# Nine output slots for the experts' rows in place of three, and one set of load semaphores for two stages

## The reference, cut to what matters

```python
xn = _layernorm(x, axis=-1)
x = x + gnn(xn, edge_index, edge_attr_64, ...) + mix(xn[None], ...)[0]   # segment sums + MLP; 4 layers of linear attention + MLP
x = x + ffn(_layernorm(x, axis=-1)[None], ...)[0]
```

```python
logits = xf @ router_w.T + router_b
idx = jnp.argmax(logits, axis=-1)
w1t = jnp.take(W1, idx, axis=0)
h = jnp.einsum('nd,ndh->nh', xf, w1t) + jnp.take(b1, idx, axis=0)      # 256 -> 64
h = jax.nn.relu(h)
w2t = jnp.take(W2, idx, axis=0)
out = jnp.einsum('nh,nhd->nd', h, w2t) + jnp.take(b2, idx, axis=0)     # 64 -> 256
out = jax.nn.relu(out)
```

## Time and profile before

| | |
|---|---|
| Runs before, us | 3072.39, 3080.54, 3084.48; median 3080.54 |
| Time of the profiled execution, us | 3077.36 |
| Its span, us | 3075.2 |
| Busy, share of the span | PE 88%, DVE 69%, ACT 50%, POOL 56% |
| Mean granted clock of PE | 0.938 |
| Stage of the experts' segments | about 2880 to the end |

### The profile page before, as it was taken

How to read it: one execution, slowest core, us unless ns; L and a number is a source line. 1 busy time by engine, 2 the same in 40 slices (tenths; PEclk the granted TensorE clock), 3 DMA queues, 4 the chain that set the end, 5 groups by cost and what they waited for, 6 DMA issues and landing times.

```text
span 3075.2 us, 56118 instructions
## 1 busy us (share of the span) xinstructions
PE 2715.3 (88%) x18842; PEld 2482.9 (81%) x18842; DVE 2125.2 (69%) x4836; ACT 1528.0 (50%) x2947; POOL 1723.8 (56%) x1611
## 2 busy tenths in 40 slices
PE   4888899999979999997999999788888888992597
PEld 2666799999978999996889999688888888992465
DVE  8887567677756666675567767688888886893144
ACT  0333366666635566662565666344444445771254
POOL 0011178777758888885888885154454553224455
PEclk7898899999989999998999999799999998996688
DMA  3000223323232223223223221233323322201332
GB/s 119 24 27 25 82 50 68 68 61 64 54 93 66 63 68 65 59 62 95 64 59 68 65 64 43 64 108 84 87 81 87 82 81 60 59 25 50 85 100 76
DMA packets 255488, 207.87 MB, mean 68 GB/s; under 512 B 165433, under 2 KB 194314, under 8 KB 255205
## 3 DMA queue, kind: packets, MB, share of 16 engines
q1 hardware_dynamic: 197606, 162.55, 19.7%
q0 software_dynamic: 57600, 41.75, 7.0%
HBM read 136.93 MB, written 70.16 MB: 67 GB/s over the span
## 4 chain that ended last, share of the span: by engine, by line
PE 18%; POOL 13%; issue 8%; DVE 7%; DMA 4%; ACT 2%; DVEq 1%; SPq 0%; POOLq 0%; ACTq 0%
PE bank L375 16%; POOL edges_sorted L725 8%; DMA nodes_out<-orow,oidx 3%; POOL tokens_sorted L790 2%; DVE xh L1266 2%; PE bank L1808 1%; DVE hidh_lo L1302 1%; DMA staging<-in_edge_attr 1%; POOL r L703 1%; DVE oh L1494 1%; POOL ehl L742 1%; DVE bn L1257 1%; ACT hidh_hi L837 1%; ACT ehl L913 1%; ACT hid L831 0%
## 5 line engine op out<-in xcount | busy, mean ns | idle before, releaser
L725 POOL DMA_INDIRECT edges_sorted<-staging,pos_i x850 | 1058.2, 1245 | 254.2 <-issue 230.8
L831 ACT ACTIVATE hid<-bank,b1p 128x250 f32<-128x250 f32 x800 | 331.9, 466 | 388.0 <-PE bank L375 385.8
L375 PE MATMUL bank<-h_hi,w_hi 128*128 128x250 f32 x1600 | 482.7, 302 | 19.7 <-DVE h_lo L1286 19.7
L1302 DVE TENSOR_TENSOR hidh_lo<-hid,hidh_hi 128x500 fp32r<-128x500 f32 x400 | 296.9, 742 | 272.6 <-ACT hidh_hi L837 265.1
L375 PE MATMUL bank<-w_hi,hidh_hi 128*125 128x256 f32 x1600 | 468.1, 293 | 0.0
L375 PE MATMUL bank<-h_hi,w_lo 128*128 128x250 f32 x1600 | 451.1, 282 | 0.0
L375 PE MATMUL bank<-w_hi,hidh_lo 128*125 128x256 f32 x1600 | 450.9, 282 | 0.0
L375 PE MATMUL bank<-w_lo,hidh_hi 128*125 128x256 f32 x1600 | 449.8, 281 | 0.0
L375 PE MATMUL bank<-h_lo,w_hi 128*128 128x250 f32 x1600 | 448.0, 280 | 0.0
L375 PE MATMUL bank<-wqk,h 128*125 128x256 f32 x1600 | 380.6, 392 | 0.6 <-ACT mbc L882 0.6
L375 PEld LDWEIGHTS bank<-wqk,h 128*125 128x125 f32 x1600 | 306.3, 195 | 47.4 <-issue 1.2
(11 more groups left out here) (289 smaller groups left out, 5754.5 us busy)
## 6 DMA issues: line engine op xcount, KB each, us to landing
staging<-edges_sorted SPq DMA_DIRECT2D x103, 260.0 KB, 2.7
staging<-in_edge_attr SPq DMA_DIRECT2D x50, 531.2 KB
queries<-qn SPq DMA_DIRECT2D x100, 250.0 KB
qin<-queries SPq DMA_DIRECT2D x100, 250.0 KB
edges_sorted<-staging,pos_i POOLq DMA_INDIRECT x850, 3.7
rows_in<-edges_sorted SPq DMA_DIRECT2D x50, 260.0 KB, 2.7
yin<-tokens_sorted SPq DMA_DIRECT2D x81, 127.0 KB
raw<-in_L_mix_W SPq DMA_DIRECT2D x8, 1024.0 KB, 6.3
```

The source lines that it names most:

```text
L375: return nc.tensor.matmul(o, left, right, start=start, stop=stop, skip_group_check=True)
L725: nc.gpsimd.indirect_dma_start(out=edges_sorted, out_offset=bass.IndirectOffsetOnAxis(ap=pos_i[:, i:i + 1], axis=0), in_=stage[:, slot, j, ...
L831: a = nc.scalar.activation(hid[c % 2][:, j, :], chunks(PH[c % 2])[:, j, :], ACT.Gelu, bias=b1p[:, 2 * c + j:2 * c + j + 1])
L1302: nc.vector.tensor_tensor(hidh[c % 2][1][:, :, :], hid[c % 2][:, :, :], f32(hidh[c % 2][0][:, :, :]), ALU.subtract).then_inc(f_lo, 1)
```

## The change

`OUTS` becomes 9: nine slots each of `orow` and `oidx`, with nine semaphores `F_OUT` made in a list. 81 is divisible by 9, so POOL's waits at the end become nine waits for 16 * 9 in place of three for 16 * 27. The twelve semaphores `F_IN` and the six `S_IN` become one list of twelve, `ROWS_IN`. The edges' six slots use its first six, and the sorted rows' twelve slots all of it; the values that are waited for in the experts' stage count the edges' loads of that slot as well. A helper `segments` that nothing calls goes.

```diff
-OUTS = 3
+OUTS = 9
@@
-        S_IN = [ctx.enter_context(nc.semaphore(f"s_in{i}")) for i in range(RIN)]
+        ROWS_IN = [ctx.enter_context(nc.semaphore(f"rows_in{i}")) for i in range(YIN)]
@@
-        F_IN = [ctx.enter_context(nc.semaphore(f"f_in{i}")) for i in range(YIN)]
@@
-        f_row, f_idx, f_out0, f_out1, f_out2 = sems("f_row f_idx f_out0 f_out1 f_out2")
+        f_row, f_idx = sems("f_row f_idx")
+        F_OUT = [ctx.enter_context(nc.semaphore(f"f_out{i}")) for i in range(OUTS)]
@@
-        N_IN, F_OUT = [n_in0, n_in1], [f_out0, f_out1, f_out2]
+        N_IN = [n_in0, n_in1]
@@
+        def edges_in(n):
+            return ROWS_IN[n % RIN], 16 * (n // RIN + 1)
+
+        def tokens_in(n):
+            slot = n % YIN
+            return ROWS_IN[slot], 16 * (len(range(slot, ESEGS, RIN) if slot < RIN else ()) + n // YIN + 1)
@@ load_segment
-                          ...).then_inc(S_IN[n % RIN], 16)
+                          ...).then_inc(edges_in(n)[0], 16)
@@ SP, the segments' loads
-                sp.dma_start(yin[n % YIN][:, :], ...).then_inc(F_IN[n % YIN], 16)
+                sp.dma_start(yin[n % YIN][:, :], ...).then_inc(tokens_in(n)[0], 16)
@@ POOL seg_low, and ACT likewise
-                pool.wait_ge(S_IN[n % RIN], 16 * (n // RIN) + 16)
+                pool.wait_ge(*edges_in(n))
@@ ACT, experts
-                    act.wait_ge(F_IN[i % YIN], 16 * (i // YIN + 1))
+                    act.wait_ge(*tokens_in(i))
@@ DVE, experts
-                    dve.wait_ge(F_IN[n % YIN], 16 * (n // YIN + 1))
+                    dve.wait_ge(*tokens_in(n))
```

More of the change, by code:

```diff
@@ L495, in load_segment @@
             eng.dma_start(rows_in[n % RIN][:, :, :],
-                          edges_sorted[bass.ds(first, SEG), :].rearrange("(p r) c -> p r c", r=SEGR)).then_inc(S_IN[n % RIN], 16)
+                          edges_sorted[bass.ds(first, SEG), :].rearrange("(p r) c -> p r c", r=SEGR)).then_inc(edges_in(n)[0], 16)
         block_ = ctx.enter_context(nc.Block())
@@ L665, in _ @@
                     sp.wait_ge(f_idx, 2 * (n - YIN + 1))
-                sp.dma_start(yin[n % YIN][:, :], tokens_sorted[bass.ds(first, P), :]).then_inc(F_IN[n % YIN], 16)
+                sp.dma_start(yin[n % YIN][:, :], tokens_sorted[bass.ds(first, P), :]).then_inc(tokens_in(n)[0], 16)
         @block_.gpsimd
@@ L909, in seg_hi @@
                     act.wait_ge(q_out, 16 * ALL)
-                act.wait_ge(S_IN[n % RIN], 16 * (n // RIN) + 16)
+                act.wait_ge(*edges_in(n))
                 if n >= 4:
```

## The result

| | before | after |
|---|---|---|
| Median of 6 timed runs, us | 3081.07 (3072.39 to 3084.48) | 3055.80 (3049.58 to 3061.65) |
| After / before | | 0.9922, 95% interval 0.9907 to 0.9937 |
| Time of the profiled execution, us | 3077.36 | 3049.58 |
| First to last store, us | 174.3 | 143.6 |

The kernel became 25.3 us faster. The forecast was 3036 us, a gain of 42.8 us by the sum. In the profiled executions the difference is 27.8 us. For this first measurement the chip's number is not on record, nor whether both profiles came from one chip.

What follows compares the result with a forecast made beforehand. The prediction took waits for output slots as the bound, then PE at 1.597 us a round. Gains of 42.4 and 0.4 us took 3077.4 to 3034.6 us, said as 3036 after a median correction; range 3026 to 3056 us (8 in 10).

Steps and rivals of the forecast that it cites:

- the sum: Last stage: 42.4 us from the 6th store on plus 0.4 us in the last four rounds, 42.8 us, giving 3034.6 us.
- The bound and the mechanism: Last stage: three slots make DVE wait for stores; nine remove this, so pace goes from 2.163 to PE's 1.597 us.
- Merged semaphores and POOL: One semaphore set costs 0; POOL's stores, at most 1.56 us each, stay under PE's 1.597 us, so 0 too.
- The loads: SP's loads for ACT in the last stage have over 4 us to spare at the faster pace; cost 0.
- a sign of being wrong: The prediction is wrong if ACT waits for loads in mid-stage; it was expected to wait only at the start.
- The end: POOL's nine final waits lie under the last landing: 0, at most 1.8 us; 4.9 us after the last store's start stays.
- The stretch at half clock ahead of the 6th store: PE's half clock from 2889.4 to 2903.0 us stays, because no slot has been used twice by then.
- Does the clock stay up: PE in the last stage: no clock falls taken, 0 us; one would cost 6.2 us, three like before 20.2 us.
- 75 x 1.597: The 75 rounds from the 6th store on at PE's full-clock pace: 119.8 us in place of 162.2, gaining 42.4 us.
- My first rival: PE's clock falls as before though the store waits go; only 22.2 us gained, 3055 us; chance 10%.
- a correction of 1.6 us: Half of the 3.2 us by which the runs' median exceeds the profiled execution, added to reach 3036 us.
- the 22.2 us of waits at full clock: PE's waits within the 162.2 us, after 119.8 us of rounds and 20.2 us of half-clock cost; all ascribed to slots.

Runs made afterwards that it cites:

- more waits: Nine slots plus already-met waits per segment (3 on SP, 5 each on DVE and ACT), against the kernel before: 0.9889 on chip 10, 0.9928 on chip 1.
- the fifth measurement: The nine-slot kernel unchanged, run on chip 11 against the kernel before: 3030.48 us, ratio 0.9870, no late hand-overs.
- the kernel with 3430 in the stage: Nine slots, PE and ACT taking expert n % 32 instead of reading the table (wrong experts' output), against the kernel before: 0.9863 on chip 10, 0.9873 on chip 1.
- the narrow stores: Nine slots storing 64 of 256 columns to another tensor, output mostly left out, against the kernel before: 0.9872 on chip 10, 0.9868 on chip 11.
- the short idle product: Nine slots, experts n % 32 without table reads, PE's idle product as one bfloat16 pass over 512 columns, against the kernel before: 0.9862 on chip 11.

## Why the prediction was right and where it failed

**The bound and the mechanism: right.** The wait for the store of three segments ago set the pace; with nine slots it is gone, DVE waits for PE, and the stores follow each other at PE's pace. On the chip without late hand-overs the unchanged nine-slot kernel takes 1.609 us a step, where 1.597 was forecast, and from the 6th store on 120.8 us where 119.4 was. The variants with nine slots on such chips take 1.593 to 1.610, and 1.661 with more waits added. Of the missing 1.4 us, one PE gap of 0.87 us is in the trace of the fifth measurement, behind a table read of 1.49 us.

**Merged semaphores and POOL: right. The loads: right in cost.** 0.9999 and 0.9998 with three slots. 1190 to 1192 ns a store. The forecast had named it as a sign of being wrong that ACT waits for loads in mid-stage, and it does: for 1.4 us in the first measurement and 8.0 in the fifth, 0.9 at most each. The pace held all the same, so the cost of 0 stands and the sign was too strict.

**The end: taken at 0, it cost 1 us.** After the last store's start come 4.9 us in the four profiled executions with three slots, 5.0 with four, 5.2 with five and 5.8 to 5.9 in the five executions of the unchanged nine-slot kernel. The step that failed here is that nothing stands behind the waits. The waits themselves do lie under the last landing, which takes 3.7 to 3.8 us in all of them. The time is in the sequencer's DRAIN instruction that ends POOL's program: from the last branch to its end 0.77 us pass with three slots, 0.93 with four, 1.10 with five and 1.75 with nine, 0.16 us for each slot. Whether the waits or the semaphores bring that was not separated.

**The stretch at half clock ahead of the 6th store: wrong, and small.** It was forecast to stay and did not come. The 6th store is at 2906.68, 1.4 us earlier than before, though the stage's scatter began 4.8 us later (2804.4 against 2799.6). No later profile has a fall ahead of its first store, those with three slots included, so this one belonged to that execution.

**Does the clock stay up, and "with the stores' waits gone I know of no gap over 1 us": this step failed.** It held the term of 0 us for falls, and, behind 75 x 1.597, the silent claim that PE has no waits left. Both are false in the measured execution:

- 135.25 us from the 6th store on in place of 119.4 are 15.8 us too many. Against the fifth measurement the whole stage is 143.6 - 128.7 = 14.9 us longer.
- By the windows 132.11 - 123.81 = 8.3 us of this is PE busy longer, most of it at half clock (14.6 x (1 - 1.597 / 2.92) = 6.6 us; the other 1.7 us I can't place), and the other 6.6 us is PE idle longer.
- Twelve of PE's idle times are over 0.3 us, 7.7 us together: eight stand behind late hand-overs, and four, 3.0 us, behind table reads of 1.3 to 1.7 us. The falls stand behind idle times of the first kind: at 2952.1 behind 0.37 and 0.69 us, at 2976.0 behind 1.14, at 3003.3 behind 0.39 and 0.68.
- With 1.0 us more at the end, 1.4 less ahead of the 6th store and 0.4 less between span and time, 15.8 makes 15.0 us, which is 3049.6 less the 3034.6 of the sum.

My first rival, the clock falls as before though the waits go, gave 3055 us and so nearly the measured median, but by luck and not by its mechanism: before's 44.5 us at half came to 13.6, and the gaps ahead of the falls are a kind that its profile didn't show. The time comes near because PE's idle time, 6.6 us, fills up part of what the clock left, and because the median of after lies 6.2 us above its profiled execution.

What could have been seen in the profile of before is very little. It has no late hand-over: that trace came from an execution that had none. The spread of the three runs, 12 us, was a hint, and I used it for a correction of 1.6 us. The table reads could have been seen: PE's took 0.31 us by the median and 1.37 at most there, and six idle times of PE, 3.5 us, stand behind long ones. So not all of the 22.2 us of waits at full clock belonged to the slots. Late hand-overs exist in before on chip 9, and cost the stage nothing that shows: from first to last store three slots take 171.2 and 172.1 us in the traces with late hand-overs and 173.6 and 174.3 in those without, while the unchanged nine-slot kernel takes 139.5 to 154.6 against 128.7. Slack hides them: a stage that waits for stores 46 to 52 times has some wherever a hand-over is late, and a stage bound by PE has none. That the slack hides them is the reading of the traces; that the same three-slot kernel has ratio 1.000 on both sorts of chip, and nine slots 0.987 on one and 0.990 to 0.992 on the other, is the measurement. The intervals partly overlap; but all four runs of the nine-slot kernel on chip 11 (3030.02 to 3030.94 us) are faster than any of its runs elsewhere (3039.54 and more).

**Open: what makes hand-overs late.** They are late updates of PE's, and they came in every profile on chips 1 and 9, in bursts, and in none on chips 10 and 11. In the same traces many semaphore updates have no record: 15 to 28 a step are there in place of 31, and no time to landing is given for the nine slots' stores. Per microsecond they hold 8.8 to 11.5 updates whatever the kernel, where the others hold 14.1 to 19.4. That looks like an upper limit on what is recorded there, and a recorder that holds engines up would be one cause; it was not shown. Every timed execution here was recorded, so an unrecorded one might have none of this. Whether the number of instructions counts is open too. By the trace, the kernel with 3430 in the stage took 4.6 us more from first to last store on chip 1 than on chip 10, that with some 4490 took 13.3 more, and the nine slots with some 4110 took 10.8 and 25.9 more than on chip 11. The fewest lost least, but the most did not lose most. Whether bytes bring late hand-overs was not shown, as the narrow stores ran on chips 10 and 11 alone.

**A better version?** Four, five and nine slots can't be told apart (0.9899, 0.9901, 0.9895). That holds for chip 1, where all three ran. No kernel that computes all of the reference was faster than nine slots beyond the spread of the runs.

## What to carry to other kernels

Give a ring of output slots the landing time, the refill and the way to the next issue, over the pace of the next bound. The refill is 0.6 us, and a store starts at the earliest 0.9 us behind the end of `orow` in the traces of before and of the fifth measurement. With the longest landing (6.6 + 0.6 + 0.9) / 1.6 gives 5.1 slots, with the median of 5.2 us 4.2. Five waited twice; four waited 33 times and did as well as nine on chip 1, at 1.7 us a step. A wait that is taken off the path also takes away the slack that hid small delays of every other hand-over, so a forecast at the next engine's bare pace can be the best case and not the middle; give the range more room on its slow side. Where a stage is kept at full clock by filler products, check in the trace how long the clock stays down after a fall, and not only whether it falls. Where a sequencer reads a table in each round, look at its longest reads and not only at the median.

## What the runs showed of the hardware that I had not expected

- The same kernel takes 3030.5 us on chip 11 and 3047.4 to 3055.8 us on chips 1 and 9 and in the first measurement, where the kernel before differs by only 3069.9 against 3073.3 to 3081.1.
- A hand-over between engines that usually takes 0.04 us behind the modelled end of a product can take up to 3 us more, while PE goes on with later products. What is late is PE's semaphore update: in the first measurement none is on record from 2950.17 to 2951.64, and then five in 0.25 us. Those of DVE and ACT that are on record there were not late.
- Once at half clock, PE stayed there for 61.4 us of work without a gap when every second round had an idle product, and for 183.0 us, busy for 181.02 of them, when none had; with one in every round it was back after 3.4 to 20.5 us.
- Falls followed idle times of PE as short as 0.69 us with another of 0.37 us 1.4 us before, while single ones of 0.87 us in the fifth measurement and 0.89 us in the earlier trace rows were followed by none. Nor were 1.14 us at 3024.4 in the first trace of after, 1.19 us at 2980.1 with the short idle product, and 1.22 us at 3005.9 with more waits on chip 1. So the length of one idle time doesn't tell whether the clock falls.
- POOL's last DRAIN took 0.16 us more for each output slot: 0.77, 0.93, 1.10 and 1.75 us with three, four, five and nine.
- A sequencer's read of one value from SBUF, 0.3 us by the median on PE, takes up to 1.3 to 2.1 us beside stores of 125 rows of 1 KB, and never 0.5 us when these are cut to 256 bytes a row (both chips on which that ran).
- With the DMA engines' share over the stage at 0.44 in place of 0.34, and nine slots in place of three, a store's landing took 5.2 us by the median in place of 4.3, and 6.6 at most as before.
